# A four-layer transformer on one core: the order of V's two halves and of a norm behind the attention scores, and one transfer instead of two for the row maxima

## The reference

```python
for layer in range(4):
    h = norm(x) * (1 + scale1) + shift1
    q, k, v = split(h @ Wqkv + b)            # 16 heads of 16 features
    if layer == 3: q, k = rope(q), rope(k)
    s = q @ k.T / 4                          # 256 x 256 per head
    if layer == 1: s = where(causal, s, -inf)
    x = x + gate1 * (softmax(s) @ v @ Wo + bo)
    h = norm(x) * (1 + scale2) + shift2
    x = x + gate2 * (act(h @ W1 + b1) @ W2 + b2)
```

## Time and profile before

| | us |
|---|---|
| median of 3 runs (lowest to highest) | 2231.6 (2230.68 to 2232.11) |
| the profiled execution, own time | 2230.71 |
| its span, first to last instruction | 2228.6 |
| PE busy | 2145.9 (96%) |
| DVE busy | 1695.1 (76%) |
| ACT busy | 1252.5 (56%) |
| POOL busy | 1043.6 (47%) |

### The profile page before, as it was taken

The page is one execution under the profiler, slowest core; times in us unless marked ns, Lnnn a source line. Parts: engine busy times, 40 slices in busy tenths (PEclk is TensorE's granted clock), DMA queues, the critical chain, the costliest instruction groups (busy, mean ns, idle before and its releaser), DMA issues.

```text
span 2228.6 us, 63249 instructions
## 1 busy us (share of the span) xinstructions
PE 2145.9 (96%) x20080; PEld 1803.2 (81%) x20080; DVE 1695.1 (76%) x4340; ACT 1252.5 (56%) x2618; POOL 1043.6 (47%) x1300
## 2 busy tenths in 40 slices
PE   5899999999999999999999999999999999999998
PEld 4688888888888888888878888888777878888887
DVE  5677777777777677767777777777788888888884
ACT  2566666666655555556666666666645454444443
POOL 2345544454545445545554554456543434343433
PEclk8899999999999999999999999999999999999999
DMA  6421222122322211222232122212222111121210
GB/s 212 152 67 64 65 71 71 63 69 84 98 71 66 73 63 59 67 75 88 87 101 66 62 67 71 68 62 76 84 76 66 59 63 65 56 72 50 73 55 25
DMA packets 164911, 166.12 MB, mean 75 GB/s; under 512 B 29440, under 2 KB 144000, under 8 KB 164800
## 3 DMA queue, kind: packets, MB, share of 16 engines
q1 hardware_dynamic: 164800, 164.69, 22.9%
HBM read 58.47 MB, written 4.39 MB: 28 GB/s over the span
## 4 chain that ended last, share of the span: by engine, by line
PE 84%; DVE 7%; SPq 3%; issue 3%; DMA 1%; POOL 1%; ACT 0%; DVEq 0%; POOLq 0%; ACTq 0%
PE B L371 35%; PE B L532 15%; PE B L701 10%; PE B L476 7%; PE B L678 7%; PE B L541 4%; DVE NEGM L1027 3%; SPq L1506 3%; PE B L551 2%; PE B L635 2%; PE B L449 2%; DVE HF L1111 0%; DMA KS<-KHL 0%; SPq L240 0%; DMA RAW<-in_w 0%
## 5 line engine op out<-in xcount | busy, mean ns | idle before, releaser
L888 ACT ACTIVATE PR<-B 128x512 f32<-128x512 f32 (+1 forms) x1024 | 505.3, 570 | 288.5 <-PE B L678 285.7
L1383 POOL TENSOR_TENSOR GHl<-G,GHh 128x256 fp32r<-128x256 f32 x512 | 377.8, 738 | 472.4 <-ACT GHh L862 289.1
L1027 DVE TENSOR_REDUCE NEGM<-B 128x2 f32<-128x512 f32 x768 | 484.7, 681 | 85.6 <-PE B L476 85.5
L371 PE MATMUL B<-H2h,W1h 128*128 128x256 f32 x1248 | 387.5, 310 | 0.0
L371 PE MATMUL B<-H2h,W1l 128*128 128x256 f32 x1248 | 353.1, 283 | 0.0
L371 PE MATMUL B<-H2l,W1h 128*128 128x256 f32 x1248 | 352.6, 283 | 0.0
L862 ACT ACTIVATE G<-B,VEC 128x256 f32<-128x256 f32 x384 | 182.3, 475 | 281.9 <-PE B L371 281.9
L532 PE MATMUL B<-W2h,GHh 128*128 128x256 f32 x1024 | 296.8, 290 | 1.7 <-POOL GHl L1383 1.7
L532 PE MATMUL B<-W2l,GHh 128*128 128x256 f32 x1024 | 290.0, 283 | 0.0
L532 PE MATMUL B<-W2h,GHl 128*128 128x256 f32 x1024 | 289.5, 283 | 0.0
L701 PE MATMUL B<-PR,V 128*32 128x256 f32 (+1 forms) x4096 | 263.1, 375 | 10.3 <-DVE HF L1111 9.4
(11 more groups left out here) (177 smaller groups left out, 4692.4 us busy)
## 6 DMA issues: line engine op xcount, KB each, us to landing
QS<-QHL SPq DMA_DIRECT2D x768, 64.0 KB, 2.1
KS<-KHL SPq DMA_DIRECT2D x768, 64.0 KB, 2.1
GA<-gate_scratch SPq DMA_DIRECT2D x48, 256.0 KB, 3.1
GM<-gate_scratch SPq DMA_DIRECT2D x48, 256.0 KB, 3.5
RAW<-in_w SPq DMA_DIRECT2D x36, 256.0 KB, 3.3
QS<-MT SPq DMA_DIRECT2D x256, 4.0 KB
GA<-in_rows_last SPq DMA_DIRECT2D x16, 256.0 KB, 3.3
GM<-in_rows_last SPq DMA_DIRECT2D x16, 256.0 KB, 3.3
```

Of the source, the lines that this page charges most:

```text
L371: last = nc.tensor.matmul(dst, w[i], x[j], start=(first_k and n == 0), stop=(last_k and n == 2))
L888: nc.scalar.activation(PR[:, h % PRING].rearrange("p k q -> p (k q)")[:, 0:n], src[:, 0:n], ACT.Exp, scale=SCALE).then_inc(ac_exp, 1)
L1027: last = nc.vector.tensor_reduce(NEGM[:, :, c], src, op=ALU.max, axis=AX.X, negate=True)
L1383: nc.gpsimd.tensor_tensor(GH[1][:, j % RING, :], G[:, j % RING, :], GH[0][:, j % RING, :].bitcast(F32), ALU.subtract).then_inc(po_gl, 1)
```

## The change

It does four things. In all layers `values(0)` is moved behind `transposed_pairs(4, 5)`, the third run. In layer 3 alone (`rope`, which is true when the next tile `s.q` is of layer 3, steps 47 to 62) `norm_2` is moved ahead of `outputs(1)`, and `values(1)` ahead of `outputs(2)`. The two DMA transfers of each half of the row maxima, 4 KB each, become one of 8 KB; the three waits on their semaphores count 16 per tile instead of 32.

```diff
@@ banks_free (PE)
-                        pe.wait_ge(sp_mt[p // HQ], 32 * (a_ + 1))
+                        pe.wait_ge(sp_mt[p // HQ], 16 * (a_ + 1))
@@ body (PE)
                     transposed_pairs(2, 3)
-                    values(0)
                     outputs(0)
                     transposed_pairs(4, 5)
+                    values(0)
+                    if rope and s.r is not None:
+                        norm_2()
                     outputs(1)
-                    if s.r is not None:
+                    if not rope and s.r is not None:
                         norm_2()
                     transposed_pairs(6, 7)
+                    if rope:
+                        values(1)
                     outputs(2)
-                    values(1)
+                    if not rope:
+                        values(1)
                     outputs(3)
@@ rows_of_maxima (ACT)
-                    at_least(ac, sp_mt[part], 32 * s.na)
+                    at_least(ac, sp_mt[part], 16 * s.na)
@@ rows_of_maxima (SP)
                     hold(ac_mt, 2 * s.a + part + 1)
-                    for half in range(2):
-                        row = ROWS * half + STK
-                        sp.dma_start(QS[row:row + 1, HQ * part:HQ * part + HQ, :].bitcast(F32),
-                                     MT[HQ * half:HQ * half + HQ, part, :].bitcast(F32)).then_inc(sp_mt[part], 16)
+                    slots = slice(HQ * part, HQ * part + HQ)
+                    sp.dma_start(QS[STK:STK + ROWS + 1:ROWS, slots, :].bitcast(F32),
+                                 MT[:, part, :].bitcast(F32)).then_inc(sp_mt[part], 16)
```

## The result

The kernel after takes 2217.55 us (median of 5 runs, 2213.94 to 2220.48) against 2231.6; the recorded ratio is 0.9944 with a 95% interval of 0.9934 to 0.9955 (the two medians alone would divide to 0.9937). The profiled execution took 2220.48 us, span 2218.3, which is 2.9 above the median of its kernel, so the two profiled executions differ by 10.2 us in time and 10.3 in span where the medians differ by 14.

A forecast was written before the change was run, and what follows sets the result against it. PE was taken to bound the kernel, 84% of the chain and busy 96% of the span. The terms -1.65 - 0.75 + 4.0 - 8.25 - 0.25 - 1.8 - 0.65 = -9.35 us gave a median of 2222.3, range 2216.5 to 2230.5.

The forecast's parts named there:

- Layer 0: Steps 1 to 15: `outputs(3)`, bound by ACT's end, starts 0.11 us earlier in each; -1.65 us, bounds 0 and -1.65.
- ACT's signal: Time from ACT's end until PE goes on, read in layer 0's fourth run and taken as 0.11 us at `outputs(3)` too.
- Layer 1: Steps 16 to 30: third run's masks just in time or 0.08 us late; net 0.05 us gained per step, -0.75 us.
- Layer 2: Steps 31 to 46: third run waits 0.36 us for K's split; 0.26 us lost in fourteen steps, +4.0 us in all.
- Leaving out step 33: Layer 2's sum counted no loss in step 33, whose chain was said to pass a load of weights, not attention.
- The second rival: Layer 2's wait doesn't cost what was said (signal earlier, or hidden by ACT's slack): -13.3 us, 2218.3; chance 0.12.
- Layer 3: Steps 50 to 62: the 0.60 us wait for L1111 goes; 0.65 us gained in 11 loop steps, -8.25 us in all.
- The step about L1111: Layer 3: DVE's L1111 can come 0.35 us earlier at most, as the rotation of K is ahead of it.
- The first rival: Layer 3: DVE takes the 8.25 us back as longer waits for NEGM; -1.1 us, 2230.5, no change; chance 0.13.
- Steps 47 to 49 and start-up: Steps 47 and 48 -0.25 us; step 49, `outputs(3)` following earlier, -1.8; SP's merged issue at start-up -0.65.
- The merged transfer: Row maxima: lands about 1.6 us after issue, asked for after 2.94; costs loop steps nothing, gains only at start-up.
- The third rival: The merged transfer lands late, so `transposed_pairs(4, 5)` waits in all 63 steps; at 3.4 us about 2251; chance 0.06.

The follow-up runs named there:

- run 3: The kernel after, but V's first half stays ahead of `outputs(0)` while the next tile is of layer 2; 0.9924 of the kernel before, layer 2 step 31.65 us.
- run 4: The kernel after without its two moves in layer 3, V's first half still moved; 0.9991 of the kernel before, layer 3 step 38.45 us.
- run 5: The kernel after with other banks in layer 2 for heads 10, 11, 14, 15 and the norm; 0.9921 of the kernel before, layer 2 step 31.47 us.
- run 6: The kernel after, but layer 0 splits Q and K by layer 2's two longer operations, biases zero; 0.9974 of the kernel before, layer 0 step 31.78 us.
- run 7: The kernel after, but in layer 3 the norm is behind `outputs(1)` again, V's second half still moved; 0.9963 of the kernel before, layer 3 step 37.78 us.
- run 8: The kernel after, but in layer 3 V's second half is behind `outputs(2)` again, the norm still moved; 0.9961 of the kernel before, layer 3 step 37.95 us.
- the first experiment: First of the runs: the kernel before with only the merged transfer of the row maxima and its three waits, PE's order old; 1.0001 of the kernel before.
- run 9: The kernel of run 5 with the norm directly behind V's first half, ahead of `outputs(1)`, in all layers; 0.9878 of the kernel before.
- run 2: The kernel after with two transfers of the row maxima per half again, the changed order kept; 0.9952 of the kernel before.
- run 10: The kernel of run 9 with V's second half ahead of `outputs(2)` in all layers; 0.9865 of the kernel before.

## Why the prediction was right, point by point

What each layer would do was right, and runs 3 to 8 show it. That the total, -9.35, came so near to the -10.3 of the traces is in part luck. The terms of the four layers add up to -6.65; the traces show -9.9 for them (-2.2, -1.5 without step 17, +4.1 without step 33, -10.3). The other terms, -2.7, can't be found, and steps 17 and 33 differ by 1.1 us net in favour of the kernel after, mostly for reasons that are not the edit.

**Layer 0.** Mechanism right, size off: 0.17 us a step for 0.11. The mis-sized term is ACT's signal, which I put at 0.11 us, read at the second pair of the fourth run, where PE goes on 0.11 after ACT's end. At `outputs(3)` it takes 0.05. With that, 350.93 - (350.71 + 0.05) = 0.17. Over the stretch from 2 to 15 this gives the 2.2 us.

**Layer 1.** The masks wait 0.09 us for the heads, close to the 0.08 that I had held possible. The step gained 0.09 and not 0.05, inside the bounds. The stretch as a whole shows -0.3 because of step 17.

**Layer 2.** The new wait is 0.36 us, as written, and the step grows by 0.28 for 0.26. Two errors cancel in that size: the gap moves what stands behind it by 0.45 and not 0.36, and ACT's signal takes 0.05 and not 0.11, so 0.26 + 0.09 - 0.06 = 0.29. The stretch without step 33 makes +4.1 for +4.0. Leaving out step 33 was wrong: it is 32.9 to 33.0 us in all six traces with the early run and the old banks in layer 2, and 32.6 in the first experiment. Runs 3, 5 and 6 remove the wait in two ways and produce it in another layer. The second rival, that it costs nothing, is refuted.

**Layer 3.** 0.84 us for 0.65, and -10.3 for -8.25. Two terms were too small. The norm behind V saves 0.15, which I had mentioned as 0.1 and not put into the sum (run 7 against the kernel after: 37.78 - 37.63; run 9 in the other layers); half of V doesn't last 0.90 us "wherever it stands", but 0.72 ahead of the norm. And ACT's signal is again 0.04 to 0.05 instead of 0.11. With both, 0.60 + 0.15 + 0.06 = 0.81. The step about L1111 was slightly off as well: I let it come 0.35 us earlier at most, as it couldn't start before the rotation of K had ended, though the two rows are 1795.22 - 1794.80 = 0.42 apart. It came 0.50 earlier (7.70 us into the step, which starts at 1784.96, for 8.20), for the row starts at 1792.66, ahead of the end of the rotation at 1791.87 + 0.86 = 1792.73. The first rival, DVE taking the gain back, did not come: PE's waits for NEGM at L1032 are 10.1 us in 18 times, against 11.0 in 18 before.

**Steps 47 to 49 and start-up.** These terms, -0.25, -1.8 and -0.65, can't be confirmed. From the start of step 47 to that of step 50 the twelve traces show 111.7 to 115.1 us, in no relation to the edit: 113.2 before, 113.0 after, 112.2 with the transfer alone, 115.1 with the order alone. And step 47 was misread: in the kernel before its chain goes from the split of K through five issues to the landing, and not through the 12 issues of Q as that of step 48 does. What varies is seen in the chain of the kernel after in step 47, where one of SP's 17 issues takes 1.82 us in place of 0.59, and K lands 20.7 us into the step instead of 19.7:

```profile
1574.10 1.82 SPq L1510
...
1577.24 2.09 DMA KS<-KHL
```

Step 49 went from 43.36 to 41.90, near the 1.8 of the sum, but the transfer alone, with the old order, shows 41.75 at a granted clock of 1.00. At a clock of 0.96 over the step, the old order took 43.36, only V's first half moved 42.25, and the full order 41.6 to 41.9 in seven traces. That fits a gain that exists only where the clock falls; one trace of the old order at 0.96 is too little to settle it. Start-up: step 0 began 2.9 us later in the kernel after. The merged transfer isn't on the chain up to there; the granted clock was lower ahead of it, 0.61 from 40 to 55 us where before it was 0.78 from 40 to 52, and one group of 16 matmuls (L419) took 1.87 us instead of 1.00. From there to step 2 the kernel after was 2.2 shorter, but the kernel with the order alone and two transfers was 1.7 shorter as well, and with the merge the other traces show anything from 0.5 to 2.2. So the merge isn't shown to be the reason, and this is left open.

**The merged transfer.** Costed at nothing in the steps, and nothing it was. The third rival, that it lands late, is refuted by runs 1 and 2 and by the packets.

The remainder between traces and medians, 10.3 us against 14, is of the size by which runs of one kernel differ (6.5 us among the five of the kernel after). The ratio of 0.9944 is worth 12.5 us, and the larger sets of runs beside the experiments put the kernel before at 2228.8 to 2230.6 and not 2231.6, so 14 is at the high end.

## What to carry to other kernels

When a call is moved ahead, list for every resource that it takes when that resource becomes free in each variant of the loop body: one kind of layer had 0.4 us to spare at the same bank where another was 0.36 us late, and the better answer was another bank there, not the old order. Before costing a removed stop, find the wait that ends next behind it; here it was ACT's last four heads, and a move that doesn't bring these forward gave nothing (run 10). Calls of one array shape belong side by side, but this too pays only ahead of what the bounding engine waits for (run 9 against run 10). And terms at places where DMA issues or the clock vary by more than the term shouldn't be read from one execution.

## What the runs showed of the hardware that I had not expected

PE went on 0.11 us after the end of DVE's or ACT's instruction at a bank, and 0.04 to 0.05 us after ACT's end at `outputs(3)`; I had taken one figure for both. Two calls of the same array shape side by side save 0.15 us against the same two with a call of 32 columns between them. A gap of 0.36 us among weight loads cost 0.45 us of the step. A transfer of 8 KB, in 8 data packets and 2 small ones, had passed within 1.75 us of its issue. Now and then one of SP's issues takes 1.8 us in place of 0.59 (1.79 in step 33 before, 1.82 in step 47 after), and what waits for the transfers behind it is late.
